# Attention heads of a post-LN transformer layer: probabilities in two buffers instead of three, matmuls with V no longer one key block late, the next query projection spread wider and its rotation moved to the end of the head

## The reference, cut to what matters

```python
x = _layernorm(x + _L0_attn_ref(x, W_q, W_k, W_v, W_o))      # 4 x 2048 x 2048
x = _layernorm(x + _L0_ffn_ref(x, W0, bias0, W1, bias1))
# attention: 16 query heads, 4 key/value heads, head size 128
Q, K, V = x @ W_q, x @ W_k, x @ W_v
Qr, Kr = _apply_rope(Q), _apply_rope(K)                      # rotary positions
weights = softmax(Qr @ Kr.T / sqrt(128))                     # per head, 2048 x 2048
out = (weights @ V) @ W_o
# feed-forward: hidden size 8192, exact gelu
```

## Time and profile before

| what | us |
|---|---|
| median of 2 runs | 1948.58 |
| the two runs | 1948.57 and 1948.59 |
| the profiled execution | 1947.27 |
| its span on the slowest core (core 0) | 1945.7 |
| spans of the 8 cores | 1933.7 to 1945.7 |

### The profile page before, as it was taken

The page is one execution under the profiler, slowest core; times in us unless marked ns, Lnnn a source line. Parts: engine busy times, 40 slices in busy tenths (PEclk is TensorE's granted clock), DMA queues, the critical chain, the costliest instruction groups (busy, mean ns, idle before and its releaser), DMA issues.

```text
span 1945.7 us, 19157 instructions; the slowest of 8 cores (1933.7 to 1945.7 us)
## 1 busy us (share of the span) xinstructions
PE 1594.7 (82%) x6912; PEld 666.4 (34%) x6912; DVE 606.6 (31%) x548; ACT 494.7 (25%) x513; POOL 447.8 (23%) x412
## 2 busy tenths in 40 slices
PE   0198887877778777698399999999999999999950
PEld 0043332222223222243044444444444444444410
DVE  0002355556565664012803021120303122120318
ACT  0011155656565564123310100101010100101070
POOL 5000054444444444000710010101001010100006
PEclk9999989898989898898599999999999999999985
DMA  9900111010101004552324455534345454422004
GB/s 123 164 17 1 44 22 33 11 22 12 22 12 22 1 1 70 125 130 65 50 44 79 87 87 87 87 53 74 55 80 87 87 87 87 76 49 49 1 1 173
DMA packets 45162, 115.61 MB, mean 59 GB/s; under 512 B 5392, under 2 KB 7440, under 8 KB 45072
## 3 DMA queue, kind: packets, MB, share of 16 engines
q0 software_dynamic: 39744, 96.49, 30.3%
q1 hardware_dynamic: 5328, 17.90, 2.4%
HBM read 202.45 MB, written 8.39 MB: 108 GB/s over the span
## 4 chain that ended last, share of the span: by engine, by line
PE 68%; DVE 12%; POOL 6%; another core or an unknown queue 5%; issue 4%; ACT 4%; DMA 1%; DVEq 0%; ACTq 0%; POOLq 0%
PE ps L894 23%; PE ps L872 22%; POOL slot L619 6%; PE ps L763 6%; PE ps L665 5%; DVE slot L629 5%; PE ps L363 3%; PE ps L387 3%; PE ps L511 2%; ACT slot L646 2%; PE ps L633 2%; DMA slot<-wo 1%; DVE slot L849 1%; DVE slot L942 1%
## 5 line engine op out<-in xcount | busy, mean ns | idle before, releaser
L872 PE MATMUL ps<-slot 128*128 128x512 bf16 x2048 | 452.3, 383 | 32.5 <-ACT slot L857 32.5
L894 PE MATMUL ps<-slot 128*128 128x512 bf16 x2048 | 443.3, 379 | 0.0
L902 DVE TENSOR_TENSOR slot<-slot,ps 128x1024 f32<-128x1024 f32 x112 | 136.8, 1222 | 633.7 <-PE ps L894 631.5
L646 ACT ACTIVATE slot<-ps 128x1024 bf16<-128x1024 f32 x256 | 257.5, 1021 | 205.3 <-DVE slot L629 97.9
L872 PEld LDWEIGHTS ps<-slot 128*128 128x128 bf16 x2048 | 199.6, 98 | 285.1 <-issue 47.6
L894 PEld LDWEIGHTS ps<-slot 128*128 128x128 bf16 x2048 | 200.4, 98 | 241.6
L619 POOL TENSOR_TENSOR slot<-slot 128x1024 f32<-128x1024 f32 x96 | 221.4, 2306 | 257.5 <-ACT slot L646 252.2
L880 ACT ACTIVATE slot<-ps,b0fm 128x1024 bf16<-128x1024 f32 x64 | 71.3, 1114 | 750.7 <-PE ps L872 750.7
L511 PE MATMUL ps<-slot 128*128 128x512 bf16 x512 | 166.6, 415 | 80.2 <-ACT slot L646 76.5
L629 DVE TENSOR_TENSOR slot<-slot 128x1024 f32<-128x1024 f32 x144 | 187.7, 1304 | 39.7 <-ACT slot L646 31.2
L633 PE MATMUL ps<-slot 128*128 128x512 bf16 x512 | 167.0, 410 | 15.9 <-ACT slot L646 15.8
(11 more groups left out here) (80 smaller groups left out, 800.8 us busy)
## 6 DMA issues: line engine op xcount, KB each, us to landing
slot<-w POOLq DMA_DIRECT2D x128, 256.0 KB, 13.5
...
```

The costliest lines, as they stand in the source:

```text
L646: em.op("sc", (lambda ptp=ptp, sb=sb: SC.activation(pt_ap(ptp, 0, Q), PT[sb][:, 0:Q], AF.Exp, scale=SCALE)), reads=[PS[2 * sb], PS[2 * sb ...
L872: grp.add((lambda ncl=ncl, qb=qb, dc=dc, par=par: T.matmul(PT[par][:, qb * QBW:(qb + 1) * QBW], w0_ap(dc, ncl * 128, (ncl + 1) * 128), x1b ...
L894: grp.add((lambda dc2=dc2, qb=qb, ncl=ncl, par=par: T.matmul(PT[2 + par][:, qb * QBW:(qb + 1) * QBW], w1_s[ncl]["bf"][:, dc2 * 128:(dc2 + ...
L902: em.op("dv", (lambda dc2=dc2, par=par: DV.tensor_add(racc[dc2]["f32"][:, 0:Q], racc[dc2]["f32"][:, 0:Q], PT[2 + par][:, 0:Q])), reads=av_ ...
```

## The change

It does five things to the loop over heads:

1. The matmuls with V and the addition of block `kc` stand right behind the exponential of the same block, not behind that of the next one (`av_den` is gone).
2. There are two buffers of probabilities, chosen by `kc % 2`.
3. The query projection takes four matmuls in each of the blocks 6 to 13, not seven in each of 6 to 9 and four in block 10. (`n_slots_q` is 10, so `per` is 4 and the 32 matmuls end at block 13.)
4. The rotation of both halves (`qrope_block`) stands after block 15, before the next head.
5. The rotated queries have a `Buf` for each of the four places instead of one for each pair.

Nothing is computed in another way, and no instruction is added or dropped.

```diff
+    qr_bufs = [Buf(f"qr{i}") for i in range(4)]
+    def qr_buf(h):
+        return qr_bufs[h % 4]
...
-    pt_s2 = pool.take()
-    pt_h = [Buf("ptA"), Buf("ptB"), Buf("ptC")]
+    pt_h = [Buf("ptA"), Buf("ptB")]
...
-                reads=[kr_s[g]["buf"], qr_s[(h // 2) % 2]["buf"]],
+                reads=[kr_s[g]["buf"], qr_buf(h)],
...
-    QPROJ_AT = tuple(range(6, 11))
+    QPROJ_AT = tuple(range(6, 13))
...
         for kc in range(KC):
             if kc + 1 < KC:
                 st_emit(h, kc + 1)
             sb = kc % 2
-            ptp = kc % 3
+            ptp = kc % 2
+            ptlo = ptp * 1024
...
-            if kc > 0:
-                av_den(kc - 1)
+            for qb in range(NQB):
+                avgrp.add((lambda kc=kc, g=g, qb=qb, par=par, ptlo=ptlo: T.matmul(
+                    PT[2 + par][:, qb * QBW:(qb + 1) * QBW],
+                    v_ap(kc, g),
+                    pt_s["bf"][:, ptlo + qb * QBW:ptlo + (qb + 1) * QBW],
+                    start=(kc == 0), stop=(kc == KC - 1))),
+                    reads=[vt_s[kc // 4]["buf"], pt_h[ptp]],
+                    last=(kc == KC - 1 and qb == NQB - 1))
...
-                if qgrp[0] is not None and QPROJ_AT[0] <= kc <= QPROJ_AT[-1]:
+                if qgrp[0] is not None and kc >= QPROJ_AT[0]:
                     n_mem = DC * NQB
-                    n_slots_q = len(QPROJ_AT)
+                    n_slots_q = KC - QPROJ_AT[0]
...
-                for qb in range(NQB):
-                    if kc == QPROJ_AT[-1] + 1 + 2 * qb:
-                        qrope_block(qh, qb, other_lo)
-        av_den(KC - 1)
...
         if qh < H:
-            if KC < 14:
+            if KC <= QPROJ_AT[0]:
                 qproj_rope(qh, other_lo)
+            else:
+                for qb in range(NQB):
+                    pa = qb % 2
...
+                    em.op("dv", (lambda qb=qb, qlo=qlo, pt_i=pt_i: DV.tensor_mul(
+                        scr2["bf"][:, qlo:qlo + QBW],
+                        PT[pt_i][:, qb * 512:qb * 512 + QBW],
+                        st_s["bf"][:, qb * QBW:(qb + 1) * QBW])),
+                        reads=[PS[other_lo + qb], st_s["buf"]], writes=[scr2_h[pa]])
```

More of the change, by code:

```diff
@@ L559, in tail_stage @@
                 writes=[attn_s[h // 2]["buf"]])
[L561 to L581, removed]
-            PT[pt_i][:, qb * 512:qb * 512 + QBW],
-            st_s["bf"][:, qb * QBW:(qb + 1) * QBW])),
-            reads=[PS[other_lo + qb], st_s["buf"]], writes=[scr2_h[pa]])
-        em.op("dv", (lambda qh=qh, qb=qb, qlo=qlo: DV.tensor_add(
-            qr_ap(qh, qb * QBW, (qb + 1) * QBW),
-            qr_ap(qh, qb * QBW, (qb + 1) * QBW),
-            scr2["bf"][:, qlo:qlo + QBW])),
-            reads=[qr_s[(qh // 2) % 2]["buf"], scr2_h[pa]],
-            writes=[qr_s[(qh // 2) % 2]["buf"]])
     qproj_rope(0, 4)
@@ L608, in build_program @@
         avgrp = None
-        dv_first = [min(kc for kc in range(KC) if kc not in POOLSET)]
+        dv_first = True
         em.op("g", (lambda par=par: GP.memset(den_pl[par]["f32"][:, 0:Q], 0.0)),
@@ L679, in build_program @@
         if qh < H:
-            if KC < 14:
+            if KC <= QPROJ_AT[0]:
                 qproj_rope(qh, other_lo)
+            else:
+                for qb in range(NQB):
+                    pa = qb % 2
+                    qlo = pa * 1024
+                    pt_i = other_lo // 2
+                    em.op("sc", (lambda qb=qb, qlo=qlo, pt_i=pt_i: SC.activation(
+                        scr2["bf"][:, qlo:qlo + QBW],
+                        PT[pt_i][:, qb * 512:qb * 512 + QBW], AF.Copy)),
+                        reads=[PS[other_lo + qb]], writes=[scr2_h[pa]])
+                    em.op("pe", (lambda qb=qb, qlo=qlo, pt_i=pt_i: T.matmul(
+                        PT[pt_i][:, qb * 512:qb * 512 + QBW], swap_sb.ap(),
+                        scr2["bf"][:, qlo:qlo + QBW],
+                        start=True, stop=True)),
+                        reads=[bswap, scr2_h[pa]], writes=[PS[other_lo + qb]])
+                    em.op("dv", (lambda qh=qh, qb=qb, qlo=qlo: DV.tensor_mul(
+                        qr_ap(qh, qb * QBW, (qb + 1) * QBW),
+                        scr2["bf"][:, qlo:qlo + QBW],
+                        ct_s["bf"][:, qb * QBW:(qb + 1) * QBW])),
+                        reads=[scr2_h[pa], ct_s["buf"]],
+                        writes=[qr_buf(qh)])
+                    em.op("dv", (lambda qb=qb, qlo=qlo, pt_i=pt_i: DV.tensor_mul(
+                        scr2["bf"][:, qlo:qlo + QBW],
+                        PT[pt_i][:, qb * 512:qb * 512 + QBW],
+                        st_s["bf"][:, qb * QBW:(qb + 1) * QBW])),
+                        reads=[PS[other_lo + qb], st_s["buf"]], writes=[scr2_h[pa]])
+                    em.op("dv", (lambda qh=qh, qb=qb, qlo=qlo: DV.tensor_add(
+                        qr_ap(qh, qb * QBW, (qb + 1) * QBW),
+                        qr_ap(qh, qb * QBW, (qb + 1) * QBW),
+                        scr2["bf"][:, qlo:qlo + QBW])),
+                        reads=[qr_buf(qh), scr2_h[pa]],
+                        writes=[qr_buf(qh)])
             if qh + 2 < H:
@@ L693, in build_program @@
     dump("attn0", lambda: attn_ap(0, 0, Q), attn_s[0]["buf"], [128, Q])
-    for b, sl in zip(pt_h, (pt_s, pt_s, pt_s2)):
+    for b in pt_h:
+        if b.last_w is not None:
+            pt_s["buf"].readers.append(b.last_w)
+        pt_s["buf"].readers.extend(b.readers)
+    for i, b in enumerate(qr_bufs):
+        sl = qr_s[i // 2]
         if b.last_w is not None:
```

60 lines of the change are left out of this document (24 added, 36 removed).

## The result

| | before | after |
|---|---|---|
| median, us | 1950.35 of 12 runs | 1956.56 of 13 runs |
| ratio, 95% interval | 1 | 1.0035 (1.0024 to 1.0045) |
| the profiled execution | 1947.27 | 1959.58 |
| spans of the 8 cores | 1933.7 to 1945.7 | 1938.9 to 1958.0 |

The changed kernel is slower by 0.35%, some 7 us, where I had forecast +2.

The account below looks back on a forecast made before the run. Heads were taken as bound by waits. Heads 1 to 13 -2.0, head 0 -1.9, head 14 +2.2, head 15 +3.5 sum to +1.8 on 1947.3; with 1.3 for the median, 1950.4 us, range 1938 to 1966.

Parts of the forecast that it names:

- The signs named ahead: Trace signs: exp(0) wait some 1.2 us, ended by scores; longer GpSimd waits, shorter VectorE waits; heads 1 to 13 at 32 to 33.
- Stage C: End of a head, exp(15) to the next head's exp(0): 5.46 us falls to 3.2 to 3.3, gaining 2.2.
- Stage B: Middle of a head, first projection matmul to exp(15): 16.15 us falls to 14.15, gaining 2.0.
- Stage A: Front of a head, exp(0) to the first projection matmul: 11.51 us grows to 14.6, costing 3.1.
- Rival 1: Front of the head costs +2.0, not +3.1, as short rotation steps and GpSimd do not meet: 1936 us; chance 0.13.
- Rival 3: At the head's front VectorE, with copy L524, queues behind GpSimd: 3.3 us a head, 1995 us; chance 0.05.
- Rival 4: The head's end and middle gain fully, its front costs only 1.5 us: -38 us, 1912; chance 0.03.
- the clock adds about 0.25: Heads 1 to 13: lower TensorE clock at the front adds 0.25 us each, beside 0.3 for the working's shortfall against the trace.
- Rival 2: TensorE clock at 1.2 GHz for most of the front of every head: +14 us, 1964; chance 0.19.
- Heads 0, 14 and 15: Heads priced apart from 1 to 13: head 0 -1.9 us, head 14 +2.2, head 15 to the output projection +3.5.
- The finer buffers for rotated queries: Five finer buffers release nothing on the path, since rotation is done a head ahead of its use: nothing.
- The output projection and its loads move as a block: nothing: After head 15: w0 loads still wait for the softmax sums, so the change there is between 0 and 1 us.

Follow-up runs that it names:

- a4_rot14: The changed kernel with four buffers of probabilities and both halves of the rotation behind block 14; 1.0030 of the time before, +6 us.
- a_mid_prompt: The changed kernel with the projection back at seven matmuls a block and the rotation back at blocks 11 and 13; 1.0124 of the time before, +24 us.
- b2_two_buffers: The kernel before with two buffers of probabilities and nothing else changed; 1.0263 of the time before, +51 us.
- b4_four_buffers: The kernel before with four buffers of probabilities and nothing else changed; 1.0057 of the time before, +11 us.

## Why the prediction was right, and where it was off

- **Within 2%, slightly slower:** right. The time, 1956.6, lies in the range 1938 to 1966 and 0.6 us above the forecast's own range of 1943 to 1956. Part of this closeness is luck: the heads cost 15.0 us in the profiles where the sum has 1.8, and two gains that the sum put at nothing (start of head 0, output projection) gave 5.2 back.
- **The signs named ahead:** the wait before exp(0), its releaser, and the waits for GpSimd and for VectorE's additions came as named. Heads 1 to 13 at 33.28 us (32 to 33), the start of the projection at 15.15 (14 to 15) and head 15 at +4.6 (2 to 4) lie a little outside.
- **Stage C, 3.2 to 3.3 us:** 3.16 in the head shown and on the mean. The wait went, and what I had named as next is next.
- **Stage B, 14.15:** 14.64 in the head shown, where GpSimd gates as worked out and four of the eight steps are some 0.1 longer; 14.98 on the mean. The gain is not 2.0 but 0.84 a head. The one head of before that I cut had 16.15 us there; the mean is 15.82.
- **Stage A, 14.6:** 15.34 in the head shown, 15.15 on the mean. The steps are those of the text: the third rotation step is held by addition 0 (1.60 where it takes 0.43), the tail's addition by addition 1, over at 7.02 where I had 6.70. From there the matmuls of the tail run at 1.2 GHz: the two sum matmuls take 1.01 us, where a pair at full clock takes 0.22 + 0.38.
- **Rival 1, that the short rotation steps don't meet GpSimd:** refuted, 903 ns against 426.
- **Rival 3, that L524 waits for GpSimd:** refuted. The copy (L522 now) takes 1.21 us in the middle of GpSimd's additions, while L525 behind it, with both inputs in SBUF, takes 2.01. But one SBUF input can be enough to wait. The cast of VectorE's first block (L602 in the versions with four buffers) takes 0.68 to 0.70 us where no GpSimd addition runs, and 2.61 beside them. Its row in a4_rot14, core 2, duration in ns, min/median/max:

```profile
L602 DVE CAST slot<-slot x16: 679/2606/2609, 243.6 to 738.4; 128x1024 f32<-128x1024 bf16 x16
```

The Trainium skill's "SBUF — State Buffer", section "SBUF: two separate sides", names both kinds: a VectorE instruction in a two-port performance mode, or with two SBUF inputs against a GpSimd instruction that reads SBUF, needs the shared pair. These traces agree on the addition and on the copy that reads PSUM. In which mode the cast runs, no view shows.
- **Rival 4:** refuted, A lost 3.8 us, not 1.5, in the head shown and on the mean.
- **The term that failed: "the clock adds about 0.25".** It was mis-sized. With the clock at 1.00 heads 1 to 13 take 32.56 on the mean, doubled matmuls included; my own working without the clock gave 32.0 + 0.3 = 32.3. With the clock as it is they take 33.28. So the clock is worth at least 0.72 us a head, 0.47 more than I took, 13 x 0.47 = 6 us of the 9.5 by which these heads missed. (This takes it that doubling the matmuls did nothing but hold the clock.) The other 3.4 is 0.26 a head of steps that I had too short: with the clock held, B is 14.68 where I had 14.15 and A 14.73 where I had 14.6, and the 0.3 that I had added without a place covers about half of that. Rival 2 had the mechanism at +14 for the extreme in which the clock is down in every head; it is down on the path in some. I averaged a clock over a stage, but what it costs depends on whether the low stretch covers the few matmuls for which everything waits, and I had the rows for that (0.53 over 6.8 us) before me. The Trainium skill's "TensorE: Matmul & The Clock Gate", section "A second HAM failure mode: psum-queue depth-cycling", names the swing between the two levels where TensorE idles shortly between groups of matmuls. The trace agrees on the swing: 1.00, 0.73, 0.50 and 0.75 in the pieces of the longer head.
- **Heads 0, 14 and 15:** signs right, each 1.0 to 1.6 us too low. No run here looked into them alone; with four buffers head 15 is back at its old length, head 14 gets 1.3 of its 3.8 us back.
- **The finer buffers for rotated queries, put at nothing:** wrong by 3.1 us. (They are four.) The prediction looked at the loop, where the rotation is done a head ahead of its use. In front of the loop the rotation of head 1 stood between head 0 and its first scores.
- **"The output projection and its loads move as a block: nothing":** wrong by 3 us in the kernel's favour. Two w0 loads no longer wait for the softmax sums, and whether they are the cause stays open. a_mid_prompt, with the old places of projection and rotation, has two early loads and 139.5 us; b2_two_buffers has none and 144.8; b4_four_buffers has two and 142.5, a4_rot14 two and 144.4.

Why it moved the time so little: of some 51 us that the third buffer was worth, the earlier readers and the later rotation and projection gave back 44. In the head shown above, B and C win 1.5 + 2.3 = 3.8 us and A loses 15.34 - 11.51 = 3.8, since rotation, tail and GpSimd's additions now meet on VectorE while TensorE runs short of work and loses its clock.
